# Reordering GpSimd's program in a hybrid attention, FFN and S4D layer: weights rounded first and in pieces, the S4D taps last

## What is computed

```python
def reference(...):                       # x is (2, 512, 256)
    x = x + attn(layernorm(x))            # batch by batch, causal, one head of width 256
    x = x + ffn(layernorm(x))
    x = x + s4d(layernorm(x))             # causal convolution with a kernel from 8 modes a channel
    x = x + ffn(layernorm(x))             # the same weights again
    return x

def attn(x):                              # normalises again, gamma and beta
    q, k, v = x_norm @ qkv[:, :256], x_norm @ qkv[:, 256:512], x_norm @ qkv[:, 512:]
    return softmax(where(causal, q @ k.T / 16, -inf)) @ v @ o_proj + x

def ffn(x):                               # gate_w, up_w: (256, 768); down_w: (768, 256)
    mm = lambda x, w, scale: (x @ w.astype(float8_e4m3fn).astype(x.dtype)) * scale
    return mm(silu(mm(x, gate_w, gate_scale)) * mm(x, up_w, up_scale), down_w, down_scale)
```

## Time and profile before

| | |
|---|---|
| runs | 141.25, 141.35 and 142.14 us, median 141.35 |
| the profiled execution | its span, first to last instruction, is 140.5 us; no other time of it is known |
| median less span | 0.85 us |
| mean granted clock of TensorE | 0.942 |
| busy, share of the span | PE 84%, DVE 75%, POOL 71%, ACT 44% |

### The profile page before, as it was taken

The page is one execution under the profiler, slowest core; times in us unless marked ns, Lnnn a source line. Parts: engine busy times, 40 slices in busy tenths (PEclk is TensorE's granted clock), DMA queues, the critical chain, the costliest instruction groups (busy, mean ns, idle before and its releaser), DMA issues.

```text
span 140.5 us, 2050 instructions
## 1 busy us (share of the span) xinstructions
PE 118.3 (84%) x650; PEld 78.2 (56%) x650; DVE 105.1 (75%) x244; ACT 62.3 (44%) x117; POOL 100.1 (71%) x156
## 2 busy tenths in 40 slices
PE   5489999999999700899999999794999896999950
PEld 5466587585877400785456844453745465446640
DVE  0459999998885896059735699999999998656272
ACT  3124156532331103644795437394454474374500
POOL 6282899998899998997864175669879883029621
PEclk9968999999999995559999999999999999999996
DMA  3999700000000020000000000000000000001304
GB/s 129 281 320 361 225 3 7 2 0 0 0 1 0 0 71 4 7 0 0 0 0 0 0 0 0 2 0 0 0 0 0 0 0 5 0 0 40 109 0 149
DMA packets 5599, 6.03 MB, mean 43 GB/s; under 512 B 900, under 2 KB 4952, under 8 KB 5592
## 3 DMA queue, kind: packets, MB, share of 16 engines
q1 hardware_dynamic: 5464, 5.91, 12.8%
q0 software_dynamic: 128, 0.03, 0.1%
HBM read 4.89 MB, written 1.05 MB: 42 GB/s over the span
## 4 chain that ended last, share of the span: by engine, by line
PE 29%; DVE 29%; POOL 25%; issue 6%; ACT 4%; DMA 3%; SPq 1%; POOLq 0%; DVEq 0%; ACTq 0%
PE psum L1064 15%; PE psum L1077 7%; POOL s4d L304 5%; DVE stats L594 4%; PE psum L1002 3%; DMA x_in<-in_x 3%; DVE fused L843 3%; DVE scaled_down L791 3%; POOL rstd L280 3%; DVE h_rows L832 3%; PE psum L1025 2%; POOL gate L390 2%; POOL up L390 2%; POOL gate_raw L386 2%; POOL up_raw L386 2%
## 5 line engine op out<-in xcount | busy, mean ns | idle before, releaser
L408 POOL TENSOR_TENSOR f_tail<-fused,f_head 128x512 f16<-128x512 f32 x12 | 14.6, 1219 | 15.2 <-ACT f_head L560 15.2
L549 ACT ACTIVATE gated<-psum,scales 128x512 f32<-128x512 f32 x24 | 16.3, 681 | 15.0 <-PE psum L1064 15.0
L1077 PE MATMUL psum<-down,f_head 128*128 128x256 bf16 x96 | 22.0, 273 | 0.1
L1077 PE MATMUL psum<-down,f_tail 128*128 128x256 bf16 x96 | 22.0, 273 | 0.0
L843 DVE SCALAR_TENSOR_TENSOR fused<-psum,up_scales_fit,gated 128x512 f32<-128x512 f32 x24 | 17.5, 738 | 4.7 <-PE psum L1064 3.0
L560 ACT ACTIVATE f_head<-fused 128x512 f16<-128x512 f32 x24 | 15.0, 626 | 10.7 <-DVE fused L843 10.5
L1064 PE MATMUL psum<-h_head,up 128*128 128x512 f16 x48 | 14.3, 379 | 1.3 <-DVE fused L843 1.3
L850 DVE TENSOR_TENSOR f_tail<-fused,f_head 128x512 f16<-128x512 f32 x12 | 9.7, 809 | 7.1 <-ACT f_head L560 7.1
L1064 PE MATMUL psum<-h_tail,up 128*128 128x512 f16 x48 | 14.3, 379 | 0.0
L1064 PE MATMUL psum<-h_head,gate 128*128 128x512 f16 x48 | 14.3, 379 | 0.0
L1064 PE MATMUL psum<-h_tail,gate 128*128 128x512 f16 x48 | 14.3, 379 | 0.0
(11 more groups left out here) (168 smaller groups left out, 267.9 us busy)
## 6 DMA issues: line engine op xcount, KB each, us to landing
x_in<-in_x SPq DMA_DIRECT2D x4, 256.0 KB, 4.4
out<-x_in SPq DMA_DIRECT2D x4, 256.0 KB, 2.1
qkv_sb<-in_qkv SPq DMA_DIRECT2D x3, 256.0 KB, 3.9
gate_raw<-in_gate_w SPq DMA_DIRECT2D x1, 768.0 KB, 6.8
up_raw<-in_up_w SPq DMA_DIRECT2D x1, 768.0 KB, 8.6
down_raw<-in_down_w SPq DMA_DIRECT2D x1, 768.0 KB, 10.3
wo_sb<-in_o_proj SPq DMA_DIRECT2D x1, 256.0 KB, 5.1
taps_all<-taps_dram SPq DMA_DIRECT2D x1, 256.0 KB, 3.0
```

What stands on the lines that cost most here:

```text
L408: pool.tensor_tensor(f_tail[:, m, :], fused[:, m % FUSED, :], f_head[:, m, :], ALU.subtract).then_inc(f_tail_by_pool, 1)
L549: act.activation(gated[:, m % 2, :], psum[:, BANK_GATE[m % 2], :], ACT.Silu, scale=gate_scales[:, m:m + 1]).then_inc(gated_ready, 1)
L1077: last = pe.matmul(column(BANK_DOWN[t // 2], H * (t % 2), H), part[:, m, t * P:t * P + P], down16[:, m, :], start=(m == 0 and t % 2 == 0 a ...
```

## The change

GpSimd starts on the weights right after the scales of `x_plus`, in pieces of 512 columns in place of 1536, and finishes all three before the first `inverse_std` of the attention's output; `make_taps` is cut in three parts that stand between later steps. ScalarE takes `x_plus` (`add_norm`) and the squares of gate and up (`square_weights`), and GpSimd waits for each of these squares before it changes the weights in place. VectorE no longer squares; it makes the three grids earlier, the bound at tile 5 and `fit_powers` at tile 6, and it searches the rounded weights for the largest magnitude in FFN pass 0 (`largest_weight`). The NaN mark is summed by TensorE in pass 2 and applied by VectorE there (`void_beyond`). TensorE's loop over passes 0 to 2 is written out. Much shortened:

```diff
 # GpSimd (pool): the order of its program
-            for k in range(K):
-                pool.tensor_scalar(x_plus[:, k, :], x_in[:, k, :], one_rstd[:, k:k + 1],
-                                   neg_mean_rstd[:, 0, k:k + 1], ALU.mult, ALU.add).then_inc(x_plus_ready, 1)
-            make_taps()
-            for w, rounded in ((0, gate16), (1, up16)):
-                step(add_grid(w))
-                pool.tensor_tensor(flat(rounded), flat(raws[w]), grid[w][:], ALU.subtract).then_inc(gate_up_ready, 1)
-            inverse_std(1, 0, 2, negative_mean=True)
-            inverse_std(1, 2, 2, negative_mean=True)
-            mark(add_grid(2))
+            pieces = [slice(S * n, S * n + S) for n in range(C * I // S)]
             for w, rounded in ((0, gate16), (1, up16)):
+                for part in pieces:
+                    if part.start == 0:
+                        pool.wait_ge(grid_ready, w + 1)
+                        pool.wait_ge(squares_ready, w + 1)
+                    mark(pool.tensor_tensor(flat(raws[w])[:, part], flat(raws[w])[:, part], grid[w][:, part], ALU.add))
+                settle()
+                for part in pieces:
+                    last = pool.tensor_tensor(flat(rounded)[:, part], flat(raws[w])[:, part], grid[w][:, part], ALU.subtract)
+                last.then_inc(gate_up_ready, 1)
+            pool.wait_ge(grid_ready, 3)
...
+            inverse_std(1, 0, 2, negative_mean=True)
             pool.wait_ge(bound_squared, 1)
             pool.tensor_tensor(bound[:, 4, :], bound[:, 3, :], pos_half[:], ALU.pow).then_inc(bound_ready, 1)
-            settle()
-            step(pool.tensor_tensor(flat(down_q), flat(down_raw), grid[2][:], ALU.subtract))
+            taps_begin()
+            inverse_std(1, 2, 2, negative_mean=True)
             pool.wait_ge(fit_ready, 1)
             for m in range(M):
                 pool.tensor_scalar(down16[:, m, :], down_q[:, m, :], bound[:, 6, m:m + 1], 1.0, ALU.mult,
                                    ALU.mult).then_inc(down_ready, 1)
-            for k in range(T, K, 2):
-                inverse_std(1, k, 2, negative_mean=True)
+            inverse_std(1, T, 2, negative_mean=True)
+            taps_middle()
+            inverse_std(1, T + 2, 2, negative_mean=True)
+            taps_end()
 # ScalarE (act)
+            def square_weights(w):
+                act.wait_ge(w_loaded[w], 16)
+                act.activation(square[w][:], flat(raws[w]), ACT.Square).then_inc(squares_ready, 1)
+            def add_norm(k):
+                act.wait_ge(x_plus_scales_ready, 1)
+                act.activation(x_plus[:, k, :], x_in[:, k, :], ACT.Identity, scale=one_rstd[:, k:k + 1],
+                               bias=neg_mean_rstd[:, 0, k:k + 1]).then_inc(x_plus_ready, 1)
...
+            square_weights(0)
             exp_scores(0)
             g_part(1)
+            square_weights(1)
             exp_scores(1)
             copy_probs(0)
             v_part(1)
+            for k in range(T):
+                add_norm(k)
             for k in range(2, K):
                 exp_scores(k)
                 copy_probs(k - 1)
+                if k < 2 + T:
+                    add_norm(k + 2)
 # VectorE (dve)
-            def weight_square(w):
-                mark(dve.tensor_tensor_reduce(square[w][:], flat(raws[w]), flat(raws[w]), 1.0, 0.0, ALU.mult, ALU.max, max_square[:, w:w + 1]))
+            def largest_weight(w):
+                rounded = (gate16, up16, down_q)[w]
+                mark(dve.tensor_reduce(largest[:, w:w + 1], flat(rounded), AX_X, ALU.max, apply_absolute_value=True))
+            def void_beyond():
+                dve.wait_ge(beyond_summed, 1)
+                dve.tensor_scalar(beyond[:, 1:2], psum[:, BANK_H[0], 0:1], 0.0, 3e38, ALU.is_gt,
+                                  ALU.mult).then_inc(beyond_read, 1)
+                dve.wait_ge(beyond_read, 1)
+                step(dve.tensor_scalar(beyond[:, 2:3], beyond[:, 1:2], 3e38, None, ALU.mult))
+                step(dve.tensor_tensor(beyond[:, 3:4], beyond[:, 2:3], beyond[:, 2:3], ALU.subtract))
+                step(dve.tensor_scalar(down_scale_all[:], down_scale_all[:], beyond[:, 3:4], None, ALU.add))
...
             for k in range(2, K):
                 row_max(k)
-                if k == 3:
-                    weight_grid(2)
-                if k == 4:
-                    mark_beyond()
+                if k == 5:
+                    read_norms()
+                    bound_gate_up()
                 if k == 6:
-                    read_norms()
-                if k == 7:
-                    bound_gate_up()
+                    fit_powers()
                 attention_out(k - 2)
             attention_out(K - 2)
             h_tails(0)
-            fit_powers()
             attention_out(K - 1)
...
                     tail(n, 2)
+                    if n == 2:
+                        void_beyond()
                     x3_stats(second)
...
+                        if n == 0 and m == 3:
+                            dve.wait_ge(gate_up_ready, 2)
+                            largest_weight(0)
+                        if n == 0 and m == 4:
+                            largest_weight(1)
+                    if n == 0:
+                        dve.wait_ge(down_ready, M)
+                        largest_weight(2)
+                        mark_beyond()
 # TensorE (pe)
-                if k == 5:
+                if k == 4:
                     channel_norms()
...
+                    if n == 2 and m == 1:
+                        pe.wait_ge(beyond_ready, 1)
+                        pe.matmul(column(BANK_H[0], 0, 1), ones[:], beyond[:, 0:1], start=True,
+                                  stop=True).then_inc(beyond_summed, 1)
...
-            with pe.Fori(0, 2 * B - 1) as n:
+            for n in range(2 * B):
                 ffn_pass(n)
```

77 lines of the change are left out of this document (40 added, 37 removed).

## The result

The changed kernel takes 144.01 us (median of five executions, 143.21 to 146.3) against 141.72 of the kernel before in the same session: ratio 1.0176, interval 1.014 to 1.0213. It is slower by 2.3 us; 143.7 had been forecast. The ratios in this document leave out the executions that were over 1.5% slower than the fastest one of the same kernel, and the medians have them all.

What follows compares the result with a forecast made beforehand. The prediction took GpSimd's weight work, which delays the attention's shifts and leaves TensorE a hole before tile 7, as the bound, then VectorE in passes 1 and 2. Terms -2.0 + 2.8 + 1.6 = +2.4 gave 143.7 us, range 140.1 to 145.5.

Steps and rivals of the forecast that it cites:

- Part 1: Up to the FFN's start (F): GpSimd rounds earlier, F moves by -2.0 us, bounds -4.3 and -0.8.
- Part 2: FFN pass 0: three searches over 1536 columns on VectorE, partly in idle time, cost +2.8 us, bounds +0.6 and +3.4.
- I cost the cut into pieces at nothing: GpSimd's rounding: pieces queued without waits add nothing to six passes of 3.43 us; at 0.05 a piece, 0.9.
- The hold-up under the third grid and the small ones: GpSimd's rounding: the third grid on VectorE costs it 1.9 us more, the small instructions 0.3.
- the queue behind `fit_powers`: VectorE and ScalarE before tile 7's turn: work queued behind the wait for the bound takes 3.6 us, turn at 55.0.
- The gap: TensorE before tile 7's turn: still idle some 5 us, longer than the 4.1 after which the clock fell.
- the rival of two elements a cycle: Pass 0: the searches' reductions run twice as fast and cost +0.6 us, total 141.5; chance 0.08.
- Part 3: Pass 2: `void_beyond`, four dependent instructions ahead of `x3_stats` on VectorE, costs +1.6 us, bounds +0.9 and +1.9.
- Part 4: Hidden work: the taps end near 68.5 us, about when GpSimd's first tail is due; back from DRAM near 81.
- The lock: Shared port of VectorE and GpSimd, held per instruction: VectorE's bound waits for pieces of 1.15 us rather than 3.43.
- 0.85 us between span and time: Whole kernel: the median lies 0.85 us above the profiled span of 140.5, so 2.4 added to 141.35 gives 143.75.
- the unchanged clock: TensorE's gap before tile 7: clock doesn't fall if the gap stays under 4.1 us; 141.4 us, chance 0.20.

Runs made afterwards that it cites:

- filling: The changed kernel with 36 extra transposes of the identity on TensorE in its hole before the turn of tile 7: 143.48 us, ratio 1.0129.

## Why the prediction was right

The sum was +2.4 us, in three terms. The stretches show each: +2.2 in all, and each mechanism as forecast. That the sum is so close is partly luck: Part 1 was 0.55 us worse than forecast and Part 2 0.6 better.

**Part 1, when F comes: -1.45, forecast -2.0, bounds -4.3 and -0.8.** The mechanism was right step by step: the rounding starts 1.70 us behind o (forecast 1.68), by ACT's square of 1.48 (1.5). The root ends 28.69 us behind o and not 27.5. The step that was mis-sized is "I cost the cut into pieces at nothing": three pieces take 3.72 us, and with whole instructions the root came 1.9 sooner. The hold-up under the third grid and the small ones had been put at 2.2 and was 1.3, which took part of it back. From the root to tile 7's turn it was 3.56 us (3.6), so the queue behind `fit_powers` was read rightly. The gap was 6.4 us where "5 us" was said, by the later root, and the clock fell. So the turn came only 0.5 us sooner than before, counted from o, where 1.7 was forecast. Two thirds of the gain in F is the clock's: the turn to F took 6.41 us against 7.37, where the forecast had put 7.0. Here too two errors, 1.2 and 0.6, go against each other.

**Part 2, pass 0: +2.19, forecast +2.8, bounds +0.6 and +3.4.** A search takes 1.74 us for 16-bit and 1.75 for 32-bit inputs. So the rival of two elements a cycle is wrong. This agrees with the Trainium skill, "VectorE: DVE Perf Modes", section "The perf-mode tier table (the rule you actually need)", which has `tensor_reduce` at the same, lowest rate (1x) for bf16 and fp32. (That rival was also priced too high: its +0.6 halves all three searches, though the third reads 32-bit values; with two halved it would be some +1.1.) The miss is in the surroundings: `fuse(0, 3)` ended at F+9.5 and not F+10.0.

**Part 3, pass 2: +1.49, forecast +1.6.** The subtraction waited for GpSimd's tail, 0.74 us in all, as feared. What the prediction missed is what the longer wait of PE behind it (2.9 us, 1.4 before) does: in six of the eight profiles with whole `void_beyond` in pass 2 and PE not filled there, the clock fell at the start of pass 3 and cost 1.1 to 2.7 us behind h3. In after's own profile it did not; that its other executions lost some there is argued from their records alone.

**Part 4** held: the taps ended at 68.91 us (forecast 68.5), and POOL's first tail started at 69.55 after 0.64 us of waiting for ACT. The taps were back from DRAM at about 82.2 us, and DVE's first use of them is at 88.2.

**The lock.** DVE's three 128x6 products in the bound, 1.81, 0.17 and 3.38 us before, took 0.87, 1.19 and 1.30 beside pieces of 1.24: none waits longer than one GpSimd instruction. With whole instructions one of the three took 3.34 and the other two 0.17 and 0.15. That agrees with the exclusive lock in the Trainium skill, "SBUF — State Buffer", section "SBUF: two separate sides". But the sum hardly differs, 3.36 us in pieces and 3.66 whole, since each product can wait for a piece of its own; only the third grid gains clearly, 3.9 against 5.8 us. The pieces cost GpSimd 1.9 us for that, and the ratios with and without them are the same, 1.0176 and 1.017.

**The sum against the median.** I took 0.85 us between span and time, from a median that wasn't the profiled execution's; where both are known it is 1.8 to 2.1. The profiled execution of before would thus be some 142.4 (an estimate, 140.5 + 1.9), above its median. The error drops out of the forecast, which adds +2.4 to the median. It hides something, though: the profile of before is one of its longest executions. Its mean granted clock is 0.942, and of 52 others of this kernel three have 0.941 and the rest 0.948 to 0.969. So the -1.45 us of Part 1 is measured against a hole in which the clock was low for longer than usual, as far as the means tell. The terms, +2.2 together, stand against +2.3 of the medians; that they agree is not a proof of each.

Of the rivals, the unchanged clock didn't come, though it would have been worth the 2.0 us that filling showed. Its condition was wrong: "if the gap stays under 4.1 us" would not have saved it, since the clock also fell in or just behind gaps of 2.3 to 3.2 us. What stays open: why the clock fell 2.2 us into the gap in one kernel and 3.8 us into the same gap in another, and why it held in two profiles with 2.9 us of waiting ahead of pass 3. ScalarE's new work (`add_norm`) and PE's loop written out were not tested by themselves.

## What to carry to other kernels

An instruction ahead of which another engine's result is awaited carries everything queued behind it: ask where a step that nobody needs yet (a mark of four small instructions, a search) can stand with no one behind it. The same four steps cost 1.5 us at one place and nothing at another. And when a gap in front of TensorE changes length, price the clock with it: keeping it was worth 2.0 us here, nearly as much as the three searches, and several edits that did what they should were paid back there. A profile is one execution; where the clock falls in some and not in others, compare stretches and not spans.

## What the runs showed of the hardware

- Cutting a GpSimd instruction over 1536 columns in three costs 0.3 us (3.72 against 3.43).
- The clock and a wait of PE ahead of the turn of tile 7: it held with 1.69 and 1.70 us, and fell in waits of 2.32, 2.55, 2.82, 3.18, 6.4 and 8.27, or just behind the restart after 2.50 and 3.19; with 36 turns of the identity ahead of a wait of 2.50 it held. Held, the turn to F took 4.39 us; fallen, 6.0 to 7.4 (7.3 and 7.5 in the two with `fit_powers` late, where the shifts of tiles 2 and 3 are waited for as well). Ahead of pass 3 it held after 1.40 to 1.43 in every profile, and with 2.90 it fell in six of eight.
- A search over 128x1536 16-bit weights on DVE beside GpSimd's rounding delays neither: 1.74 and 3.72 us, as without. A `tensor_scalar` over 128x1536 for the grid, 0.95 us in before, took 2.00 and 1.91 beside the pieces.
- The opening of PE can run at half speed while the view shows a granted clock of 1.00. PE's timeline of after, where the turns take 0.69 and 0.66 us in the kernel before, and the eight products 2.63:

```profile
4.56 1.06 PE L953 MATMUL psum<-ident,qkv_sb 128*128 128x128 f32 x4
6.93 1.11 PE L953 MATMUL psum<-ident,qkv_sb 128*128 128x128 f32 x4 [1.31 <-DMA qkv_sb<-in_qkv]
...
9.94 3.58 PE L960 MATMUL psum<-w_turned 128*128 128x256 f32 x8
```

Behind these products all that follows is 0.82 us later. Over the twelve kernels o lay between 22.43 and 24.45, and already so over the seven whose program is unchanged up to there.
